# A halving moved from VectorE to ScalarE, and the later score units ordered by halves of the batch

## The chip, the cores and the metric

The kernel runs on one core of a Trainium2 chip. The metric is the device time of one execution in microseconds (us). Before the change three executions took 118.46 us in the median (117.84 to 118.76). The core has five engines that run programs of their own and meet only at semaphores: PE (TensorE, matrix products into PSUM), DVE (VectorE), ACT (ScalarE), POOL (GpSimd) and SP (SyncE, which here only issues DMAs).

## The reference

A batch of 4 sequences of 256 tokens with 256 features is normalised (no learned scale). The normalised activations go two ways. One is attention with 16 heads of 16 features, softmax over the whole sequence, and an output projection with a bias. The other is a feed-forward layer with 1024 hidden units, exact gelu, a second bias `proj2_bias`, and silu on its result. The output is the input plus the product of the two.

```python
xn  = _layernorm(x, axis=-1)
s   = attention(xn, Wqkv) @ Wproj.T + bproj        # 16 heads, softmax over 256 keys
h   = jax.nn.gelu(xn @ proj1.T + proj1_bias, approximate=False)
g   = _silu(h @ proj2.T + proj2_bias)
out = x + s * g
```

## The kernel before

Every product of full precision is split: an operand is a high part and a low part (names in `h` and `l`), and three products are summed (the low by low one is left out). So each operand is rounded to its high part on ACT, and the low part is the difference, taken on DVE or POOL.

The silu is computed through tanh: with y half of the layer's result, silu is y * (1 + tanh(y)). For that the second bias `b2s` is needed halved. It is loaded at the start and halved in place once. POOL is the first to use it (`early_sum`, L479), DVE the next (L810); both wait for the semaphore `b2_half`.

Scores are made twice. The first time (`S` units, PE L992) they only give row maxima. There are 32 such units: unit S(2n) and S(2n+1) are the two head pairs of `PAIRS[n]` = (j, b), where b is the sequence of the batch (0 to 3) and j a group of four heads (0 to 3). A unit is four matmuls into two banks of PSUM, and one DVE reduction over 1024 columns takes the maxima (L755). Units alternate between two pairs of banks, so S(n) waits on PE until the reduction of S(n-2) is done. When all four sequences of a group j have been reduced, DVE transposes the maxima (`MT`, L761), POOL splits them (L493, L495), and eight small DMAs write them as extra rows of q. The second scores (`ST` units, L1006) come with the maxima subtracted, ACT takes their exp (L640), and `PV` units (L1039) multiply by the values.

For both kinds of scores q and k must lie stacked in `qs` and `ks`. SP does this with 48 DMAs (L422) out of `stage`, in four packs of twelve, in this order: heads j = 0, 1 of sequences 0, 1; then of sequences 2, 3; then heads j = 2, 3 of sequences 0, 1; then of sequences 2, 3. Each pack has a semaphore `stacked[half of the batch][half of the heads]`. The first `S` unit that needs a pack waits for it on PE:

```python
if s[1] % 2 == 0 and (j, b) in ((0, 0), (0, 2), (2, 0), (2, 2)):
    pe.wait_ge(stacked[b // 2][j // 2], 192)
```

What PE does, unit by unit, is a list written by `build_order`: `PLAN` names the groups of first-layer (`F1`, named R1 in pieces), second-layer (`F2`, R2) and value units (`V`, RV), and behind which pieces of a group an `S` unit is put. The `S` units are dealt out by number, so `PAIRS` alone says which heads and sequence a number stands for. All engines walk the same list and pick their own steps from it. ACT's steps in the middle are the gelu of a first-layer unit (L623), its high part (`H`, L629), the values (L601), second-layer results (L664), and from ST0 on the exps. POOL makes the low parts `hTl` (L514). The step `("F1", 4)` stands behind S5 in the list; there DVE halves `b2s` (L751).

Of the kernel before, what the change touches and what calls it, by code (L numbers as in the profile page):

```python
# [5 lines left out]
B, SQ, E = 4, 256, 256  # L6
# [7 lines left out]
FC = F // P  # L14
# [34 lines left out]
LAST = GROUPS - B  # L49
CHUNKS = (0, 2, 1, 3)  # L50
PAIRS = ([(0, 0), (0, 1), (1, 0), (0, 2), (0, 3), (1, 1), (1, 2), (1, 3)]
         + [(j, b) for j in range(2, 4) for b in range(B)])


def members(kind, p, *part):
# [88 lines left out]
def layer_kernel(nc, x, wqkv, w1, b1, w2, b2, wp, bp, out):  # L144
    f32, f32r = mybir.dt.float32, mybir.dt.float32r
    ALU, ACT, AX = mybir.AluOpType, mybir.ActivationFunctionType, mybir.AxisListType
# [6 lines left out]
    with ctx:  # L153
        def sem(name):
            return ctx.enter_context(nc.semaphore(name))
# [7 lines left out]
        def at(name, shape, dtype, where=None):  # L163
            size = 4
            for n in shape[1:]:
                size *= n
            if where is None:
                where = used[0]
                used[0] += (size + 31) // 32 * 32
                assert used[0] <= slab * 4, (name, used[0])  # L170
            return nc.alloc_sbuf_tensor_at(name, shape, dtype, offset=base + where)
# [53 lines left out]
        b2s = at("b2s", [P, E], f32)  # L225
# [17 lines left out]
        w1_in, w2_in, wp_in, bias_in = (sem(n) for n in ("w1_in", "w2_in", "wp_in", "bias_in"))  # L243
# [20 lines left out]
        f2_made, f2_out, b2_half, yh_side, yh_done, yh_part, yh_pool, th_done, gate_done, gate_part, gate_pool, bg_done, xb_done = (  # L264
            sem(n) for n in ("f2_made", "f2_out", "b2_half", "yh_side", "yh_done", "yh_part", "yh_pool", "th_done",
                              "gate_done", "gate_part",
                              "gate_pool", "bg_done", "xb_done"))
# [295 lines left out]
        @block.scalar  # L563
        def _(act):
            act.wait_ge(warm_set, 1)
            nc.scalar.activation(rc[0:1, 0, 0:1], warm[0:1, 0:1], ACT.Gelu)

            def high_wqk(c):
                act.wait_ge(wqkv_in[c], 16)
                for q in range(2):  # L570
                    nc.scalar.activation(quarter(wqh, c, q), as_loaded(c, q), ACT.Copy).then_inc(wqk_hi, 1)

            high_wqk(0)
            n_qk = n_v = n_f1 = 0
            for s in order:
                if s[0] == "XT":
                    b = s[1]
                    act.wait_ge(xt_made, b + 1)
                    for kc in range(KC):
                        nc.scalar.activation(xTh[:, kc, b * SQ:(b + 1) * SQ], bank[:, home[("XT", b)][kc], 0:SQ],  # L580
                                             ACT.Copy).then_inc(xt_hi, 1)
                    if b == 0:
                        high_wqk(1)
                        act.wait_ge(wqkv_in[2], 16)
                        nc.scalar.activation(wqh[:, 2], wqkv_raw[:, 2], ACT.Copy).then_inc(wv_hi, 1)
                elif s[0] == "QK":
                    h, i = s[1:]
                    act.wait_ge(qk_made, n_qk + 1)
                    nc.scalar.activation(stage[:, h, i, 0, :], bank_of(*s), ACT.Copy,  # L589
                                         scale=SCALE if i < 2 else 1.0).then_inc(qk_hi, 1)  # L590
                    n_qk += 1
                    if n_qk in (2, 4):
                        act.wait_ge(w1_in, 16)
                        kc = n_qk // 2 - 1
                        nc.scalar.activation(w1h[:, kc, :], w1_raw[:, kc, :], ACT.Copy).then_inc(w1_hi, 1)  # L595
                elif s[0] == "V":
                    h, p = s[1:]

                    act.wait_ge(v_made, n_v + 1 if h == 0 else 4)
                    tt = 4 * h + 2 * p  # L600
                    nc.scalar.activation(VA[:, tt:tt + 2, :, 0:HN],  # L601
                                         bank_of(*s).rearrange("p (t n d) -> p t n d", t=2, d=HN),
                                         ACT.Copy).then_inc(v_out, 1)
                    n_v += 1
                elif s[0] == "F1":
                    f = s[1] % FC
                    if n_f1 == 0:
                        act.wait_ge(w2_in, 16)
                        for fs in (slice(0, 4), slice(4, 8)):
                            nc.scalar.activation(w2s[:, fs, 0, :], w2_in_place[:, fs, 1, :], ACT.Copy).then_inc(w2_hi, 1)  # L610
                        act.wait_ge(bias_in, 48)
                        act.wait_ge(xt_made, B)
                    if n_f1 == FC:
                        act.wait_ge(f2_made, TT // 2)
                        act.wait_ge(wp_in, 128)
                        act.wait_ge(stacked[1][0], 192)
                        act.wait_ge(stacked[1][1], 192)
                        nc.scalar.activation(wph[:], wps[:], ACT.Copy).then_inc(wp_hi, 1)

                        nc.scalar.activation(rc[0:1, 0, 0:1], b1s[0:1, 0:1], ACT.Gelu)  # L620

                    act.wait_ge(f1_made, 2 * (n_f1 // 2) + 2)
                    nc.scalar.activation(hG[:, f, :], bank_of(*s), ACT.Gelu,  # L623
                                         bias=b1s[:, f:f + 1]).then_inc(gelu_done, 1)
                    n_f1 += 1
                elif s[0] == "H":
                    f = s[1] % FC
                    act.wait_ge(gelu_done, s[1] + 1)
                    nc.scalar.activation(hTh[:, f, :], hG[:, f, :], ACT.Copy).then_inc(h_hi, 1)  # L629
                elif s[0] == "ST":  # L630
                    w = s[1]
                    act.wait_ge(st_made, w + 1)
                    if w < 4:
                        act.wait_ge(stacked[0][0], 192)
                        act.wait_ge(stacked[0][1], 192)
                    if 4 <= w < 8:
                        act.wait_ge(f1_made, 2 * FC)
                    if w >= 8:
                        act.wait_ge(pv_made, (w - 8) // 2 + 1)
                    nc.scalar.activation(exp_of(w), scores_of(*s), ACT.Exp).then_inc(exp_done, 1)  # L640
                elif s[0] == "MROWS":
                    maxima_rows(act, act, 0)
                elif s[0] == "TANH" and s[1] < EARLY:
                    u = s[1]
                    act.wait_ge(yh_pool, u + 1)
                    if u >= 2:
                        act.wait_ge(gate_part, u - 1)
                    nc.scalar.activation(th[:, u % 2, :], sums_of(u)[:, 0], ACT.Tanh).then_inc(th_done, 1)
                elif s[0] == "TANH":
                    u = s[1]  # L650
                    act.wait_ge(yh_done, u - EARLY + 1)
                    if u >= EARLY + 2:
                        act.wait_ge(gate_done, u - EARLY - 1)
                    else:
                        act.wait_ge(gate_pool, u - 1)
                    nc.scalar.activation(th[:, u % 2, :], yh[:, u % 2, :], ACT.Tanh).then_inc(th_done, 1)
                elif s[0] == "F2" and s[1] < EARLY:
                    u = s[1]
                    if u == 0:
                        act.wait_ge(v_made, 4)  # L660
                    act.wait_ge(f2_made, 2 * (u // 2) + 2)
                    if u >= 2:
                        act.wait_ge(gate_pool, u - 1)
                    nc.scalar.activation(sums_of(u).rearrange("p a e -> p (a e)"), bank_of("F2", u, 0), ACT.Copy,  # L664
                                         scale=0.5).then_inc(f2_out, 1)
            for u in BY_ACT:
                store(act, act, u)
# [3 lines left out]
        def _(dve):  # L671
# [52 lines left out]
            for s in order:  # L724
                if s[0] == "XT":
                    b = s[1]
# [13 lines left out]
                elif s[0] == "QK":  # L740
                    h, i = s[1:]
# [4 lines left out]
                    n_qk += 1  # L746
                    if n_qk == 1:
                        norm_apply(3)
                elif s == ("F1", 4):
                    dve.wait_ge(bias_in, 48)  # L750
                    nc.vector.tensor_scalar(b2s[:], b2s[:], 0.5, None, ALU.mult).then_inc(b2_half, 1)  # L751
                elif s[0] == "S":
                    j, b = PAIRS[s[1] // 2]
                    dve.wait_ge(s_made, s[1] + 1)
# [2 lines left out]
                elif s[0] == "MT":  # L757
                    j = s[1]
# [16 lines left out]
                elif s[0] == "PV" and s[1] in (t[-1] for t in TOGETHER):  # L775
# [15 lines left out]
                    for n, g in enumerate(groups):  # L791
                        j, b = divmod(g, B)
# [24 lines left out]
                elif s[0] == "TURN":  # L817
                    kc, j = s[1:]
# [278 lines left out]
```

## Time and profile before

| | |
|---|---|
| median of 3 executions | 118.46 us (117.84 to 118.76) |
| profiled execution, its own time | 117.66 us |
| its span | 115.9 us |
| PE busy | 110.4 us (95%) |
| DVE busy | 87.0 us (75%), 37.8 of them the 32 reductions of L755 |
| ACT busy | 75.8 us (65%) |
| POOL busy | 71.5 us (62%) |
| PE clock granted | full in every slice |

The span is the time from the first to the last instruction of the profiled execution; its own time has 1.8 us more around it, and lies 0.80 us under the median of the unprofiled ones. Times below are from the span's start. A row of the timeline gives the start, how long the merged piece lasted, the engine, line and tile, how often (x), and in brackets how long the engine sat idle before it and what ended that. PE is the product, PEld the load of its weights, and SPq the issuing of DMAs on SP.

### The profile page before, as it was taken

The numbers are of one execution on the slowest core, as the hardware profiler recorded it, in microseconds if no ns is written. First come the engines' busy times: TensorE is split into PE (matmuls) and PEld (weight loads), VectorE is DVE, ScalarE is ACT, GpSimd is POOL, SyncE is SP. The second block draws the span as 40 slices with busy tenths as digits, with TensorE's granted clock in tenths as the row PEclk, the third lists the DMA queues.
The fourth block names the chain that finished last, engine by engine and source line by source line (L and its number), as shares of the span: only waits on it lengthen the run. The fifth ranks groups of instructions, "written<-read, shape, count | busy, mean of one in ns | idle before, by whom it ended". The sixth has DMA issues, their size and how long they took to land.

```text
span 115.9 us, 2969 instructions
## 1 busy us (share of the span) xinstructions
PE 110.4 (95%) x1114; PEld 89.2 (77%) x1114; DVE 87.0 (75%) x158; ACT 75.8 (65%) x112; POOL 71.5 (62%) x92
## 2 busy tenths in 40 slices
PE   5889999999999999999999999999999999999990
PEld 4588998779986998898788888785866867566660
DVE  0799994537889988987598899043986868999862
ACT  5074795481986630397867887979968798799100
POOL 4227679039799930099748766999691581457480
PEclk9999999999999999999999999999999999999999
DMA  3999955465613564564000001700000000020214
GB/s 96 315 358 378 344 173 194 154 209 199 206 39 100 179 198 139 193 197 132 3 7 1 6 0 69 296 0 8 7 8 10 0 0 6 0 91 6 91 47 137
DMA packets 9634, 13.30 MB, mean 115 GB/s; under 512 B 2452, under 2 KB 4884, under 8 KB 9492
## 3 DMA queue, kind: packets, MB, share of 16 engines
q1 hardware_dynamic: 9060, 12.82, 33.6%
q10 hardware_dynamic: 560, 0.30, 0.9%
q8 instruction: 9, 0.15, 0.5%
q14 instruction: 5, 0.04, 0.1%
HBM read 5.51 MB, written 1.05 MB: 57 GB/s over the span
## 4 chain that ended last, share of the span: by engine, by line
PE 55%; SPq 30%; DMA 5%; issue 3%; DVE 2%; ACT 2%; POOL 1%; POOLq 0%
SPq L422 29%; PE bank L1039 13%; PE bank L979 10%; PE bank L864 9%; PE bank L1006 8%; PE bank L1022 7%; PE bank L1019 3%; PE bank L992 3%; DMA ks<-stage 2%; DMA xs<-x 2%; PE bank L1050 2%; SPq L411 1%; PE bank L898 1%; ACT stage L589 1%; ACT w1h L595 1%
## 5 line engine op out<-in xcount | busy, mean ns | idle before, releaser
L755 DVE TENSOR_REDUCE negm<-bank 128x4 f32<-128x1024 f32 x32 | 37.8, 1218 | 7.5 <-PE bank L992 7.4
L514 POOL TENSOR_TENSOR hTl<-hG,hTh 128x512 fp32r<-128x512 f32 x16 | 20.4, 1297 | 5.6 <-ACT hTh L629 5.6
L640 ACT ACTIVATE PT<-bank 128x1024 f32<-128x1024 f32 x16 | 15.6, 1026 | 2.8 <-PE bank L1006 2.7
L623 ACT ACTIVATE hG<-bank,b1s 128x512 f32<-128x512 f32 x16 | 10.7, 681 | 7.0 <-PE bank L979 7.0
L992 PEld LDWEIGHTS bank<-ks,qs 48*128 48x128 f32 x128 | 11.8, 186 | 2.7 <-DVE negm L755 0.7
L992 PE MATMUL bank<-ks,qs 48*128 48x256 f32 x128 | 13.3, 282 | 0.3 <-DVE negm L755 0.2
L1022 PE MATMUL bank<-w2s,hTh 128*128 128x512 f32 x32 | 11.9, 410 | 0.0
L979 PE MATMUL bank<-w2s,hTh 64*128 64x512 f32 x64 | 11.9, 398 | 0.0
L979 PE MATMUL bank<-xTh,w1l 64*128 64x512 f32 x64 | 11.2, 391 | 0.0
L1006 PEld LDWEIGHTS bank<-qs,ks 50*128 50x128 f32 x128 | 8.5, 185 | 3.4 <-issue 1.2
L1006 PE MATMUL bank<-qs,ks 50*128 50x256 f32 x128 | 11.0, 297 | 0.0
L979 PE MATMUL bank<-xTh,w1h 64*128 64x512 f32 x64 | 11.0, 416 | 0.0
L629 ACT ACTIVATE hTh<-hG 128x512 fp32r<-128x512 f32 x16 | 9.9, 634 | 0.4
L979 PE MATMUL bank<-xTl,w1h 64*128 64x512 f32 x64 | 10.1, 389 | 0.0
L640 ACT ACTIVATE PT_more<-bank 128x1024 f32<-128x1024 f32 x8 | 7.9, 1025 | 1.5 <-PE bank L1006 1.5
L640 ACT ACTIVATE PT_last<-bank 128x1024 f32<-128x1024 f32 x8 | 7.9, 1025 | 1.3 <-PE bank L1006 1.3
L979 PE MATMUL bank<-w2s,hTl 64*128 64x256 f32 x64 | 8.3, 278 | 0.0
L1019 PE MATMUL bank<-w2s,hTl 128*128 128x256 f32 x32 | 8.3, 280 | 0.0
L743 DVE SCALAR_TENSOR_TENSOR stage<-bank,stage 128x512 fp32r<-128x512 f32 x8 | 5.3, 685 | 3.7 <-ACT stage L589 3.7
L533 POOL TENSOR_TENSOR bg<-gate,bps 128x256 f32<-128x256 f32 x8 | 6.4, 805 | 2.5 <-DVE gate L710 2.5
L479 POOL TENSOR_TENSOR gate<-gate,b2s 128x256 f32<-128x256 f32 x4 | 3.0, 740 | 8.0 <-ACT gate L664 8.0
L786 DVE STREAM_TRANSPOSE cd<-bank 128x256 f32<-128x256 f32 x12 | 4.9, 434 | 4.0 <-PE bank L1039 3.9
(108 smaller groups left out, 256.2 us busy)
## 6 DMA issues: line engine op xcount, KB each, us to landing
qs<-stage SPq DMA_DIRECT2D x24, 128.0 KB, 2.9
ks<-stage SPq DMA_DIRECT2D x24, 128.0 KB, 2.9
xs<-x SPq DMA_DIRECT2D x4, 256.0 KB, 3.7
w_raw<-w SPq DMA_DIRECT2D x1, 1024.0 KB, 7.4
w_in_place<-w SPq DMA_DIRECT2D x1, 1024.0 KB, 10.0
xb<-x SPq DMA_DIRECT2D x1, 1024.0 KB, 5.0
wqkv_raw<-wqkv SPq DMA_DIRECT2D x3, 256.0 KB, 4.3
out<-fin SPq DMA_DIRECT2D x6, 128.0 KB, 1.8
```

The costliest lines, as they stand in the source:

```text
L422: sp.dma_start(stack[row:row + STK:3, 4 * q:4 * q + 4, cols].bitcast(f32), stage[64 * par:64 * par + 64, h, i, part, :].bitcast(f32)).then ...
L514: nc.gpsimd.tensor_tensor(hTl[:, n % FC, :], hG[:, n % FC, :], hTh[:, n % FC, :].bitcast(f32), ALU.subtract).then_inc(h_lo, 1)
L623: nc.scalar.activation(hG[:, f, :], bank_of(*s), ACT.Gelu, bias=b1s[:, f:f + 1]).then_inc(gelu_done, 1)
L640: nc.scalar.activation(exp_of(w), scores_of(*s), ACT.Exp).then_inc(exp_done, 1)
L755: nc.vector.tensor_reduce(negm[:, j, :, s[1] % 2, b, :], scores_of(*s), axis=AX.X, op=ALU.max, negate=True).then_inc(max_done, 1)
L864: m = nc.tensor.matmul(dst, lhs(kc, a), rhs(kc, b), start=first and n == 0, stop=last and n == len(todo) - 1)
L979: m = nc.tensor.matmul(dst, lhs, rhs, start=first and n == 0, stop=done and not begins)
L992: last = nc.tensor.matmul(scores_of(*s)[:, par, qt, :], qs[rows, hp, c:c + P], ks[rows, hp, b * SQ:(b + 1) * SQ], start=True, stop=True)
L1006: last = nc.tensor.matmul(scores_of(*s)[:, par, kt, :], ks[rows, hp, c:c + P], qs[rows, hp, b * SQ:(b + 1) * SQ], start=True, stop=True)
L1019: m = nc.tensor.matmul(bank_of("F2", u, 0)[:, 0:E], hTl[:, fc, c:c + P], w2s[:, fc, 0, :], start=False, stop=False)
L1022: m = nc.tensor.matmul(bank_of("F2", u, 0), hTh[:, fc, c:c + P], w2s[:, fc].rearrange("p a e -> p (a e)"), start=fc == 0, stop=fc == FC - 1)
L1039: last = nc.tensor.matmul(spot("PV", g)[32 * m:32 * m + VW, :], VA[:, 2 * b + kt, 4 * j + m, :], exp_of(w)[:, m % 2, kt, :], start=(kt == ...
```

## The change

Two edits. The halving of `b2s` is no longer a DVE instruction behind S5 but an ACT instruction (a copy with scale 0.5, in place) behind the high part of hidden unit 7. And `PAIRS` lists the last sixteen `S` units as heads j = 2, 3 of sequences 0, 1 and then j = 2, 3 of sequences 2, 3, where it had all of j = 2 and then all of j = 3.

```diff
 PAIRS = ([(0, 0), (0, 1), (1, 0), (0, 2), (0, 3), (1, 1), (1, 2), (1, 3)]
-         + [(j, b) for j in range(2, 4) for b in range(B)])
+         + [(j, b) for h in range(2) for j in range(2, 4) for b in (2 * h, 2 * h + 1)])
@@ ACT
                     nc.scalar.activation(hTh[:, f, :], hG[:, f, :], ACT.Copy).then_inc(h_hi, 1)
+                    if s[1] == FC - 1:
+                        nc.scalar.activation(b2s[:], b2s[:], ACT.Copy, scale=0.5).then_inc(b2_half, 1)
@@ DVE
-                elif s == ("F1", 4):
-                    dve.wait_ge(bias_in, 48)
-                    nc.vector.tensor_scalar(b2s[:], b2s[:], 0.5, None, ALU.mult).then_inc(b2_half, 1)
```

On DVE, from the first reduction (S0) to the last transpose of maxima, before:

```order
L755 TENSOR_REDUCE negm<-bank 128x2x2 [waits s_made] x6
L751 TENSOR_SCALAR b2s<-b2s 128x256 [waits bias_in]
L755 TENSOR_REDUCE negm<-bank 128x2x2 [waits s_made] x4
L761 STREAM_TRANSPOSE mt<-negm 128x32 [waits max_done]
L755 TENSOR_REDUCE negm<-bank 128x2x2 [waits s_made] x6
L761 STREAM_TRANSPOSE mt<-negm 128x32 [waits max_done]
L755 TENSOR_REDUCE negm<-bank 128x2x2 [waits s_made] x8
L761 STREAM_TRANSPOSE mt<-negm 128x32 [waits max_done]
L755 TENSOR_REDUCE negm<-bank 128x2x2 [waits s_made] x8
L761 STREAM_TRANSPOSE mt<-negm 128x32 [waits max_done]
```

and now:

```order
L754 TENSOR_REDUCE negm<-bank 128x2x2 [waits s_made] x10
L760 STREAM_TRANSPOSE mt<-negm 128x32 [waits max_done]
L754 TENSOR_REDUCE negm<-bank 128x2x2 [waits s_made] x6
L760 STREAM_TRANSPOSE mt<-negm 128x32 [waits max_done]
L754 TENSOR_REDUCE negm<-bank 128x2x2 [waits s_made] x12
L760 STREAM_TRANSPOSE mt<-negm 128x32 [waits max_done]
L754 TENSOR_REDUCE negm<-bank 128x2x2 [waits s_made] x4
L760 STREAM_TRANSPOSE mt<-negm 128x32 [waits max_done]
```

The halving between S5's and S6's reduction is gone, and the transpose of the maxima of j = 2 stands behind S27's reduction, no longer behind S23's.

On PE, the score units S20 to S24 in the middle of the program (each is one row with its wait and one row x3; the rows between are first-layer products), before:

```order
L992 MATMUL bank<-ks,qs 128x256 [waits max_done,stacked11]
L992 MATMUL bank<-ks,qs 128x256 x3
...
L992 MATMUL bank<-ks,qs 128x256 [waits max_done]
L992 MATMUL bank<-ks,qs 128x256 x3
L979 MATMUL bank<-xTh,w1h 128x512 [waits w1_lo,w1_hi,turn_made]
```

where the first two rows are S20 and the last three S24, and now, S20 and S24 again:

```order
L991 MATMUL bank<-ks,qs 128x256 [waits max_done]
L991 MATMUL bank<-ks,qs 128x256 x3
...
L991 MATMUL bank<-ks,qs 128x256 [waits max_done,stacked11]
L991 MATMUL bank<-ks,qs 128x256 x3
L978 MATMUL bank<-xTh,w1h 128x512 [waits w1_lo,w1_hi,turn_made]
```

The wait for the last pack of stacked q and k has moved from S20 to S24; nothing else of PE's program is in another place. On ACT the new instruction stands alone between two neighbours of before:

```order
L623 ACTIVATE hG<-bank,b1s 128x512 [waits f1_made]
L629 ACTIVATE hTh<-hG 128x512 [waits gelu_done]
L631 ACTIVATE b2s<-b2s 128x256
L601 ACTIVATE VA<-bank 128x32x16 [waits v_made] x2
L378 DMA qs<-mm 2x16x32 [waits m_lo,m_hi]
```

It waits for nothing of its own, and no load of an activation table has come in with it.

## Rows read from the trace of the kernel before

**Rows 1.** The page, the chain of work that ended last, by engine
```profile
PE 55%; SPq 30%; DMA 5%; issue 3%; DVE 2%; ACT 2%; POOL 1%; POOLq 0%
```

**Rows 2.** The same chain in order of time, 44 to 58 us: start, us, what
```profile
52.78 2.85 DMA ks<-stage
...
56.18 1.38 PE bank L979 x12
```

**Rows 3.** Waits of PE's weight loads, 20 to 75 us: total, times, longest
```profile
PEld bank L992 <- DVE negm L755: 0.7, 1, 0.7
PEld bank L992 <- DMA ks<-stage: 0.4, 1, 0.4
```

**Rows 4.** Timeline of PE; the L992 rows are S6, S8, S16, S19, S20, S31
```profile
34.82 0.41 PE L992 MATMUL bank<-ks,qs 48*128 48x256 f32 x4
...
36.36 0.63 PE L979 MATMUL bank<-xTl,w1h 64*128 64x512 f32 x4
37.24 0.50 PE L992 MATMUL bank<-ks,qs 48*128 48x256 f32 x4 [0.25 <-DVE negm L755]
37.58 0.41 PE L979 MATMUL bank<-wqh,xTh 64*128 64x256 f32 x4
...
48.73 0.40 PE L992 MATMUL bank<-ks,qs 48*128 48x256 f32 x4
...
49.93 0.41 PE L1006 MATMUL bank<-qs,ks 50*128 50x256 f32 x4
...
51.35 0.40 PE L979 MATMUL bank<-w2s,hTh 64*128 64x512 f32 x2
51.59 0.40 PE L992 MATMUL bank<-ks,qs 48*128 48x256 f32 x4
...
55.20 0.39 PE L979 MATMUL bank<-w2s,hTh 64*128 64x512 f32 x2
55.68 0.50 PE L992 MATMUL bank<-ks,qs 48*128 48x256 f32 x4
56.02 0.63 PE L979 MATMUL bank<-xTh,w1h 64*128 64x512 f32 x4
...
70.00 0.40 PE L992 MATMUL bank<-ks,qs 48*128 48x256 f32 x4
```

**Rows 5.** Timeline of DVE, 33 to 72 us, around the halving and the transposes
```profile
33.65 1.22 DVE L755 TENSOR_REDUCE negm<-bank 128x4 f32<-128x1024 f32 x1 [0.50 <-PE bank L992]
34.79 1.26 DVE L751 TENSOR_SCALAR b2s<-b2s 128x256 f32<-128x256 f32 x1
35.97 4.71 DVE L755 TENSOR_REDUCE negm<-bank 128x4 f32<-128x1024 f32 x4
...
61.35 0.21 DVE L761 STREAM_TRANSPOSE mt<-negm 128x32 f32<-128x32 f32 x1
61.49 1.19 DVE L755 TENSOR_REDUCE negm<-bank 128x4 f32<-128x1024 f32 x1
...
64.82 7.11 DVE L755 TENSOR_REDUCE negm<-bank 128x4 f32<-128x1024 f32 x6 [0.40 <-PE bank L992]
```

**Rows 6.** Timeline of ACT, 39 to 52 us
```profile
39.02 0.63 ACT L629 ACTIVATE hTh<-hG 128x512 fp32r<-128x512 f32 x1
41.04 1.09 ACT L601 ACTIVATE VA<-bank 128x512 f32<-128x512 f32 x2 [1.38 <-PE bank L979]
...
51.64 0.41 ACT L648 ACTIVATE th<-gate 128x256 f32<-128x256 f32 x1
```

**Rows 7.** Timeline of POOL, the low parts of the first eight hidden units
```profile
32.10 8.95 POOL L514 TENSOR_TENSOR hTl<-hG,hTh 128x512 fp32r<-128x512 f32 x7 [0.37 <-ACT hTh L629]
```

**Rows 8.** Timeline of SP, the last six DMAs of the third pack
```profile
39.62 4.84 SPq L422 DMA_DIRECT2D ks<-stage  x6
```

**Rows 9.** Issue to landing of the DMAs into ks
```profile
DMA to landing us min/median/max: 2.7/2.9/3.8
```

**Rows 10.** Packets of ACT's DMA queue (the eight of L378), 48.5 to 49 us
```profile
q10 hardware_dynamic: 22, 0.00, 3.4%
```

## The prediction, made before the changed kernel was run

> **What bounds the kernel now.** I read the chain of waits first, by engine and then in order of time. By engine it gives PE 55% and SP's queue 30% [rows 1]. That 30% is easily misread. The chain is followed backwards from the end; it goes along PE down to 55.68 us, jumps there to the landing of the last stacking DMA (52.78 + 2.85 = 55.63), and follows SP's queue from there on [rows 2, 4]. So the queue is not what PE waited for all that time; it says that for some 35 us (30% of 115.9) SP issued one DMA after the other, and that PE had to stop for the last of them at one point. How long it stopped is in the waits of PE's weight loads: between 20 and 75 us there are two stops worth naming, 0.7 us for a DVE reduction and 0.4 us for that DMA [rows 3]. Otherwise PE has its next instruction ready throughout this stretch. The time is PE's own work plus its stops, and the change can only touch the stops.
>
> The timeline of PE puts the first stop at S8 (37.24) and the second at S20 (55.68) [rows 4]. S8 needs the banks that the reduction of S6 frees. The DVE timeline shows why that one was late: S5's reduction ends at 34.87, then the halving of `b2s` takes DVE until 36.05, although S6's product was there at 34.82 + 0.41 = 35.23 [rows 4, 5].
>
> **Part 1, the halving leaves DVE.** S6's reduction can start at about 35.25 where it started at 35.97. Four reductions in a row took 4.71 us, 1.18 each [rows 5], so it ends at 36.43 and not at 37.15. What PE gets of that: the piece before S8 starts at 36.36 and has four matmuls, which take a third of the 1.38 us of twelve, 0.46 [rows 2, 4]. S8 would start at 36.82. A score unit of four matmuls with 256 columns goes through in the time of two with 512, which is 0.24 (51.35 to 51.59) [rows 4]. The work behind S8 would start at 37.06; it started at 37.58. That is **0.52 us**. Bounds: 0.25, the idle time that the product row itself shows, and 0.7, that of the weight loads [rows 3, 4]. I take the spacing of the starts, since it holds what PE in fact issued later. The loads had been released at the end of the reduction, 37.15, after 0.7 us of idling [rows 3], so PE wanted S8's banks at about 36.5, 0.3 before the product. At 36.43 they are free by then, and I leave no rest of the wait.
>
> Why did 256 columns take 1.26 us on DVE, longer than a reduction over 1024? POOL had seven equal operations without a gap from 32.10 on, 8.95 / 7 = 1.28 each [rows 7]; one of them ran from 34.66 to 35.94, and the halving came free just then. The Trainium skill (SBUF — State Buffer, section SBUF: two separate sides) says that DVE in a mode that uses both ports and GpSimd take a shared pair of ports exclusively, for a whole instruction, the other blocking. By that rule the trace agrees, and the length depends on where in a POOL operation the halving falls. From the skill's table of cycles (VectorE: DVE Perf Modes, section on the TRN2 errata) I work out an estimate of 0.2 us for it undisturbed; at that length it would never have delayed S6, and the sum would lose the 0.52. The row says 1.26, and the row decides.
>
> **Part 2, S20 no longer needs the last pack.** In the new list S20 to S23 are heads j = 3 of sequences 0 and 1, which are in the third pack, the one that S16 has already waited for. S20 would have started at 55.20 + 0.24 = 55.44, and the work behind it at 55.68; it started at 56.02 [rows 4]. That is **0.34 us**; bounds 0.24 (the shift of S20's own start) and 0.4 [rows 3]. The last pack's landing is set by SP alone, so it stays at 55.63. The wait is now at S24, whose reduction started at 61.49 [rows 5], so some 5 us after the landing; it costs nothing even 0.9 us earlier.
>
> The two parts depend on each other. With part 1 alone PE would be at S20 0.52 us sooner and would wait that much longer for the same landing. Only with both does the sum 0.86 reach the end.
>
> **Part 3, the halving on ACT.** It follows the last high part, which ends at 39.65, ahead of the values, for which ACT sat idle 1.38 us until 41.04 [rows 6]. PE is 0.52 earlier now, so 0.87 us of cover is left. The price: a 256-column ACT operation took 0.41 [rows 6]; the dearest bound is the 1.26 that DVE needed [rows 5]. At 0.41 it is hidden; at 1.26 the values come 0.4 late. Queued behind them on ACT are the eight DMAs of L378, but these wait for POOL, whose row of low parts ends at 41.05 as before [rows 7]. I cost it at nothing at either end. Its users, POOL's first sum and DVE's much later one, come after second-layer work that PE finishes only about S16, 48 us [rows 4].
>
> **Part 4, the transpose of the j = 2 maxima moves behind S27.** It takes between 0.14 (start to next start) and 0.21 us [rows 5]. Where it stood, DVE was not urgent. Where it goes, six reductions run back to back from 64.82, 1.18 each [rows 5]; S29's ended at 69.56, and S31, which needs its banks, started its product at 70.00 [rows 4] and so wanted them at 69.7. The margin is 0.14 and the transpose takes 0.14 to 0.21. I take **0.02 us** lost, with 0 and 0.07 as ends. What hangs on the maxima of j = 2 (POOL's split, SP's rows) comes after POOL's second row of low parts, and ST16, the user, is late in the program.
>
> **What PE meets on its way, being earlier.** At S16 the third pack: its last six issues end at 39.62 + 4.84 = 44.46 [rows 8]. The last began about 0.8 earlier, and a landing takes 2.9 (at most 3.8) [rows 9], so it lands at 46.6, at the latest, counted from the end of the issue, 48.3. S16's product moves from 48.73 to 48.21 [rows 4]. At ST0 the eight rows of j = 0: ACT's queue still had packets after 48.5, none after 49 [rows 10]; ST0 moves from 49.93 to 49.41, its wait to 49.1. Both hold, the second by 0.1 us or a bit more. After S31 no DMA that runs by itself stands in the way: the exps, the sums and the reload of x all start from PE's products, so I let the gain pass to the end.
>
> **Sum.** -0.52 - 0.34 + 0.02 = **-0.84 us**. The profiled execution took 117.66; it becomes 116.82. The median of the runs is 0.80 above the profiled one, so I forecast 118.46 - 0.84 = **117.6 us**.
>
> **Rivals.**
>
> *Given back at a DMA.* PE's 0.52 from part 1 is lost at S16 or ST0, because the pack or the rows land later than my middle value; or S6's reduction doesn't come that much sooner. For it: the margin of 0.1 at ST0, and the upper bound of 48.3 at S16. Against: the median landing leaves 1.4 us at S16. Part 2 stays: -0.34, 118.1 us. Chance 0.20.
>
> *The stop at S20 is longer in most executions than in the profiled one.* That execution is 0.80 us under the median and under the lowest of the three. If those 0.80 lie in SP's chain of issues, the usual stop at S20 is 0.34 + 0.80 = 1.14, and the change removes it all: -0.52 - 1.14 + 0.02 = -1.64, 116.8 us. For it: the chain hung on SP for a third of the time, and its issues have no slack between them. Against: nothing shows where the scatter is; and a third pack that is over 1.4 us late would stop PE at S16. Chance 0.28.
>
> *Slower: DVE becomes the bound in S26 to S31.* Place: the six reductions, now with the transpose among them. It decides from 0.14 us of DVE lateness on, past which each tenth is lost by PE. The price, if the slip is as large as one reduction: 1.18 + 0.21 - 0.14 = 1.25 lost against 0.86 won, +0.39, 118.85 us; two reductions of slip would make it more than 1%. For it: that stretch has no idle DVE time at all. Against: DVE starts it after an idle 0.40 of its own, waiting for PE [rows 5], and PE's own order there is unchanged. Chance 0.06.
>
> *No effect at all,* since the halving's place or the wait's were not the real cause: both rows name their releaser directly, and the new order has the wait at S24; 0.04 for this and what I don't see. My forecast itself gets 0.42.
>
> **Range and chances.** The forecast's own range is 117.2 to 118.0. Reaching to the rival given back (118.1) and to the larger gain (116.8), with a few tenths for the median of few runs: 116.6 to 118.4. A difference of less than 1%, 1.18 us, can't be told from none here. Faster by more than that: nearly all of the larger gain and a tail of the forecast, 0.34. Slower by more: 0.05, from the larger slip of DVE and from what I don't see. Within: 0.61.
>
> **What would show it.** On DVE: reductions of S0 to S9 with nothing between, S6's starting within 0.1 us of its product's end. On PE: no idle before S8, none before S20, the fourth pack's wait unseen at S24. S31's product 0.8 to 0.9 us earlier than 70.00, and the end by the same amount. A new stop at S16 or ST0 would show the first rival, an idle PE before S28 to S31 with DVE as releaser the third. It is wrong in its main line if PE is earlier at S31 by what I say and not at the end: then something behind 70 us that I let follow PE has a clock of its own.

## The result

The changed kernel takes 117.1 us in the median (22 runs, 116.76 to 117.94), the kernel before in the same sessions 118.09 us (22 runs, 117.23 to 119.26). The ratio is 0.9938, 95% interval 0.9918 to 0.9958: 0.73 us faster (0.50 to 0.97). The ratio leaves out as slow the runs that are more than 1.5% above the fastest of their kernel, four of before's 22 (119.06 to 119.26), and so it gives 0.73 us where the medians of all runs differ by 0.99. Forecast were -0.84 us and 117.6 us, with a range of 116.6 to 118.4, and a change of less than 1% as the likeliest outcome. Size, sign and this range held; the narrower range that the forecast called its own, 117.2 to 118.0, missed 117.1 by 0.1, where the kernel before itself came out 0.37 under the 118.46 that the forecast started from. The way there failed in one place: a stop of PE that the prediction had at nothing. The number came out right all the same; what made up for the stop is not fully shown.

The profiled execution of the changed kernel took 117.61 us, its span was 115.8 us, so it is hardly shorter than the profiled one of before (117.66, 115.9). The two are not alike as samples: this one lies 0.51 us above the median of its 22 runs, that of before 0.43 below its own. The chain of waits, by engine:

```profile
PE 84%; DMA 5%; ACTq 4%; DVE 2%; ACT 1%; issue 1%; POOL 1%; POOLq 0%
```

SP's queue, 30% in [rows 1], is gone from it, and 4% of ACT's queue is new. The waits of PE's weight loads, 20 to 75 us, tell what happened (total, times, longest):

```profile
PEld bank L1005 <- DMA qs<-mm: 0.6, 1, 0.6
PEld bank L978 <- issue: 0.4, 1, 0.4
```

Both stops of [rows 3] are gone. There is a new one of 0.6 us, for the rows of maxima at ST0 (the 0.4 us of "issue" stands in the trace of before too). PE's timeline; the rows of L991 are S6, S8, S17, S20, S24, S30 and S31, that of L1005 is ST0:

```profile
35.03 0.40 PE L991 MATMUL bank<-ks,qs 48*128 48x256 f32 x4
...
37.02 0.40 PE L991 MATMUL bank<-ks,qs 48*128 48x256 f32 x4
37.26 0.40 PE L978 MATMUL bank<-wqh,xTh 64*128 64x256 f32 x4
...
49.37 0.40 PE L991 MATMUL bank<-ks,qs 48*128 48x256 f32 x4
50.21 0.50 PE L1005 MATMUL bank<-qs,ks 50*128 50x256 f32 x4 [0.44 <-DMA qs<-mm]
50.55 0.39 PE L978 MATMUL bank<-w2s,hTh 64*128 64x512 f32 x2
...
55.48 0.40 PE L978 MATMUL bank<-w2s,hTh 64*128 64x512 f32 x2
55.71 0.41 PE L991 MATMUL bank<-ks,qs 48*128 48x256 f32 x4
55.96 0.63 PE L978 MATMUL bank<-xTh,w1h 64*128 64x512 f32 x4
...
60.96 0.40 PE L991 MATMUL bank<-ks,qs 48*128 48x256 f32 x4
...
69.00 0.41 PE L991 MATMUL bank<-ks,qs 48*128 48x256 f32 x4
...
69.94 0.40 PE L991 MATMUL bank<-ks,qs 48*128 48x256 f32 x4
```

Against [rows 4]: this execution was 0.21 late already at S6, where nothing has changed (in the four profiled executions of before S6 starts between 34.82 and 35.16). The work behind S8 is 0.32 early, so 0.53 was won there. The work behind ST0 is late again: it would have started 0.24 + 0.24 after S17, at 49.85, and started at 50.55, 0.70 later. Behind S20 it stands at 55.96 against 56.02. The DMA that held ST0, in the chain in order of time, and the packets of its queue from 48.5 to 49 us (there are none from 49 to 49.5):

```profile
46.94 3.23 DMA qs<-mm
...
50.21 0.50 PE bank L1005 x4
```

```profile
q10 hardware_dynamic: 34, 0.00, 7.2%
```

On DVE the halving is gone and S6's reduction follows its product; the transpose of j = 2 stands in the row of reductions:

```profile
33.84 1.23 DVE L754 TENSOR_REDUCE negm<-bank 128x4 f32<-128x1024 f32 x1 [0.52 <-PE bank L991]
35.47 3.49 DVE L754 TENSOR_REDUCE negm<-bank 128x4 f32<-128x1024 f32 x3 [0.40 <-PE bank L991]
...
64.77 2.36 DVE L754 TENSOR_REDUCE negm<-bank 128x4 f32<-128x1024 f32 x2 [0.40 <-PE bank L991]
67.16 0.21 DVE L760 STREAM_TRANSPOSE mt<-negm 128x32 f32<-128x32 f32 x1
67.30 4.58 DVE L754 TENSOR_REDUCE negm<-bank 128x4 f32<-128x1024 f32 x4
```

and on ACT it takes 0.40 us, with idle time behind it:

```profile
39.76 0.40 ACT L631 ACTIVATE b2s<-b2s 128x256 f32<-128x256 f32 x1
40.72 1.09 ACT L601 ACTIVATE VA<-bank 128x512 f32<-128x512 f32 x2 [0.56 <-PE bank L978]
```

### The profile page after: what moved, and what is told of

Same layout as the page of the kernel before. It is cut to its first block, busy times and chain, and to the rows that moved or that the text cites. A ratio compares the mean times of both kernels' runs of the same rounds, so it can differ in the third digit from the quotient of the medians.

```text
span 115.8 us, 2969 instructions
## 1 busy us (share of the span) xinstructions
PE 110.5 (95%) x1114; PEld 88.9 (77%) x1114; DVE 86.0 (74%) x157; ACT 76.1 (66%) x113; POOL 71.3 (62%) x92
## 4 chain that ended last, share of the span: by engine, by line
PE 84%; DMA 5%; ACTq 4%; DVE 2%; ACT 1%; issue 1%; POOL 1%; POOLq 0%
PE bank L978 26%; PE bank L863 17%; PE bank L1038 13%; PE bank L1005 9%; PE bank L1021 7%; PE bank L991 5%; ACTq L378 4%; PE bank L1018 3%; DMA qs<-mm 3%; DMA xs<-x 2%; PE bank L897 2%; PE bank L1049 2%; ACT VA L601 1%; DVE stats L678 1%; POOL rstd L450 1%
## 5 line engine op out<-in xcount | busy, mean ns | idle before, releaser
L991 PEld LDWEIGHTS bank<-ks,qs 48*128 48x128 f32 x128 | 11.6, 186 | 2.1
L991 PE MATMUL bank<-ks,qs 48*128 48x256 f32 x128 | 12.9, 279 | 0.0
L1005 PEld LDWEIGHTS bank<-qs,ks 50*128 50x128 f32 x128 | 8.5, 185 | 4.1 <-issue 1.2
L1005 PE MATMUL bank<-qs,ks 50*128 50x256 f32 x128 | 11.1, 297 | 0.4 <-DMA qs<-mm 0.4
L500 POOL TENSOR_TENSOR w2s<-w_in_place,w2s 128x1024 fp32r<-128x1024 f32 x2 | 4.8, 2396 | 5.0 <-ACT w2s L610 5.0
```

The source lines that it names most:

```text
L991: last = nc.tensor.matmul(scores_of(*s)[:, par, qt, :], qs[rows, hp, c:c + P], ks[rows, hp, b * SQ:(b + 1) * SQ], start=True, stop=True)
L1005: last = nc.tensor.matmul(scores_of(*s)[:, par, kt, :], ks[rows, hp, c:c + P], qs[rows, hp, b * SQ:(b + 1) * SQ], start=True, stop=True)
```

## The experiments

Ratios are to the kernel before on the same chip, with their 95% interval.

### Each part alone

`halving_only` is the changed kernel with the old list of score units:

```diff
-         + [(j, b) for h in range(2) for j in range(2, 4) for b in (2 * h, 2 * h + 1)])
+         + [(j, b) for j in range(2, 4) for b in range(B)])
```

> The halving of the second bias sits on ScalarE, the score units keep their order of before. My account: PE is 0.52 us earlier from S8 on, loses that again at ST0 (waits for the rows of maxima) or at S20 (waits for the last pack of stacked q and k, landing at about 55.6 us), so the time is that of before, ratio 0.998 to 1.002. The rival 'the halving alone makes the gain' wants a ratio near 0.994 and no stop at S20.

Measured: 117.62 us, ratio 0.9983 (0.9948 to 1.0019). No difference that can be told. Its PE waits:

```profile
PEld bank L991 <- DMA ks<-stage: 0.6, 1, 0.6
PEld bank L1005 <- DMA qs<-mm: 0.2, 1, 0.2
```

S8 has no stop, and what is won there goes to a small stop at ST0 and a longer one at S20, whose product starts at 55.68 as in [rows 4].

`pairs_only` is the kernel before with the new list alone.

> The score units go by halves of the batch, the halving stays on VectorE behind S5. By my sum of one profiled execution only 0.34 us is gained (ratio 0.997) and the 0.52 of S8 stays lost. The rival 'in most executions the stop at S20 is longer than in the profiled one' wants most of the gain of the whole change here, 0.6 to 1.0 us (0.992 to 0.995), and less scatter between runs than the kernel before has. ST0 should not be stopped, since PE is not early.

Measured: 117.42 us (117.0 to 117.78), ratio 0.9962 (0.9938 to 0.9985): 0.45 us. The stop at S8 is there, those at S20 and ST0 are not:

```profile
PEld bank L992 <- DVE negm L755: 0.7, 1, 0.7
```

Between the 0.34 of one profile and the 0.6 to 1.0 of the rival this does not decide: the interval (0.18 to 0.73) holds the first and the lower third of the second. On the scatter the rival was right. The runs lie in 0.78 us, those of before in the same session in 2.0 us (117.19 to 119.20, with two far longer ones apart), and those of `halving_only`, which keeps PE's wait at S20, in 1.87.

### What the halving costs on VectorE where GpSimd is idle

`halving_dve_quiet` is the changed kernel with the halving back on DVE, behind another reduction:

```diff
-                    if s[1] == FC - 1:
-                        nc.scalar.activation(b2s[:], b2s[:], ACT.Copy, scale=0.5).then_inc(b2_half, 1)
@@ behind the reduction
+                    if s[1] == 12:
+                        dve.wait_ge(bias_in, 48)
+                        nc.vector.tensor_scalar(b2s[:], b2s[:], 0.5, None, ALU.mult).then_inc(b2_half, 1)
```

> The new order of score units, and the halving on VectorE again, but behind S12, where GpSimd has nothing to do. If the 1.26 us of before were a wait for the ports that GpSimd held, it takes 0.2 to 0.35 us here; if it is the price of the operation on VectorE, 1.26 again. Time as the changed kernel in the first case (0.993 to 0.995); in the second up to 0.5 us more if PE runs into the reduction of S14.

Its DVE timeline:

```profile
44.47 0.28 DVE L756 TENSOR_SCALAR b2s<-b2s 128x256 f32<-128x256 f32 x1
```

The same instruction takes 0.28 us here and took 1.26 in [rows 5]. In all six traces that have it behind S5 it takes 1.23 to 1.26 us and ends some 0.1 us after the end of one of POOL's low parts (at 36.05 in [rows 5], where POOL's third operation of the row ends at 32.10 + 3 * 1.28 = 35.94). The time is 117.06 us, ratio 0.9929 (0.9902 to 0.9956), as the changed kernel, with a stop of 0.4 us at ST0 like it. So what counted was to take the halving from under POOL's low parts; ScalarE is one way to do it, another place on VectorE is as good.

### The rows of maxima at ST0

`rows_shared` is the changed kernel with two of the eight row DMAs of j = 0 issued by SP (m = 3), between its third and fourth pack, and six by ACT:

```diff
-        def maxima_rows(engine, queue, j):
+        def maxima_rows(engine, queue, j, ms=range(4)):
...
-            for m in range(4):
+            for m in ms:
...
                 for h in range(2):
+                    if (q, h) == (1, 1):
+                        maxima_rows(sp, sp, 0, (3,))
...
-                    maxima_rows(act, act, 0)
+                    maxima_rows(act, act, 0, range(3))
```

> The changed kernel, with two of the eight small DMAs that write the maxima of j = 0 issued by SP between the third and the fourth pack of stacking DMAs, six by ScalarE. My account of the changed kernel's trace: PE stops 0.6 us at ST0 for the last of these rows. ScalarE's last issue would start 1.3 us earlier, so the stop goes: 0.5 to 0.6 us less than the changed kernel, ratio to before 0.989. SP's fourth pack comes 1.2 us later, landing at about 56, which S24 at 60 does not feel. If something else behind ST0 sets the end, the ratio stays at 0.994.

Measured: 116.88 us (116.67 to 117.14), ratio 0.9916 (0.9886 to 0.9946), seven runs; the profile has no stop at ST0. The expected 0.989 lies at the interval's lower end. A second measurement has the changed kernel beside it:

> The changed kernel again, beside the next one: ratio to before 0.991 to 0.996, a stop of 0.3 to 0.7 us at ST0 for the rows of maxima, none at S8 and S20.

> Two of the eight rows of maxima issued by SP, again, beside the changed kernel: 0.2 to 0.6 us less than it, the spread of its runs no wider than 0.6 us, no stop at ST0. The rival, that the difference of the first time was one between executions, wants the medians within 0.1 us of each other.

| | median us | range of 12 runs | ratio (95%) | stop at ST0 in the profile |
|---|---|---|---|---|
| `after_again` | 117.33 | 116.73 to 117.88 | 0.9954 (0.9922 to 0.9987) | 0.4 us |
| `rows_shared_again` | 116.79 | 116.69 to 117.53 | 0.9927 (0.9897 to 0.9958) | none |

PE's timeline of `rows_shared_again`; ST0, and the work behind S20 and S31 as in [rows 4]:

```profile
35.01 0.40 PE L993 MATMUL bank<-ks,qs 48*128 48x256 f32 x4
...
49.53 0.40 PE L1007 MATMUL bank<-qs,ks 50*128 50x256 f32 x4
...
55.29 0.63 PE L980 MATMUL bank<-xTh,w1h 64*128 64x512 f32 x4
...
69.27 0.40 PE L993 MATMUL bank<-ks,qs 48*128 48x256 f32 x4
```

Here the forecast's sum can be read without the new stop. S6 is 0.19 late against before and the work behind S20 0.73 early: 0.92 won, where 0.86 was forecast for the two stops. S31 is 0.73 early, and the profiled execution (116.85 us) 0.81 shorter than before's 117.66. What PE wins before 70 us does reach the end. This version is the fastest measured: medians of 116.88 and 116.79. Against the changed kernel of the same session its median is 0.54 us lower; the two ratios differ by less (0.3%) and their intervals overlap. Eleven of its twelve runs are at 117.10 us or less, and only two of the changed kernel's twelve. So that it is faster is fairly clear; the size of the step stays open, while its cause, the stop, is seen to go. One run of the twelve, 117.53, lies outside the 0.6 us that were expected for their spread.

### Delays of SP's chain, made on purpose

Two DMAs into a spare buffer, issued by SP ahead of the fourth pack, in the kernel before (`old_order_late_pack`) and in the changed one (`new_order_late_pack`):

```diff
                 for h in range(2):
+                    if (q, h) == (1, 1):
+                        for n in range(2):
+                            sp.dma_start(spare[:, n, :], bp[:, 0:16].to_broadcast([P, 16])).then_inc(spare_in, 16)
```

> The kernel before with two more small DMAs (into a spare buffer that nobody reads) that SP issues ahead of the fourth pack of stacking DMAs. If S20's wait passes every delay of SP's chain on to the end, the pack lands about 1.2 us later (two issues of 0.6) and the time grows by the same 1.2, ratio 1.010; the stop at S20 is then 1.5 us or so. If there is slack that the profile did not show, less.

> The changed kernel with the same two DMAs ahead of the fourth pack. S24 wants the pack at 60 us and gets it at 57: no stop, the time is that of the changed kernel, ratio to before 0.992 to 0.996. If the wait still binds at S24, or ScalarE's wait for the same pack (ahead of the high part of the projection's weights) delays the gelu, up to 0.5 us more.

Old order: 118.67 us, ratio 1.0074 (1.0031 to 1.0117), 0.87 us more; the 1.2 us expected lies inside the interval. Its profiled execution was the longest of its eleven runs, 121.41 us, with a stop of 2.6 us at S20, so the 1.5 expected there is not shown. It shows one thing more. PE sat idle 2.32 us until S20 at 58.02, and behind it the granted clock fell: 0.64 between 59 and 60 us, 0.50 (the lower level, 1.2 GHz) from 60 to 62, 0.66 to 63, and full again. From S20 to S24 it took 6.78 us, where [rows 4] and the start of S24 at 61.01 give 5.33. The row of S20 and the page's row of the clock:

```profile
58.02 0.51 PE L998 MATMUL bank<-ks,qs 48*128 48x256 f32 x4 [2.32 <-DMA ks<-stage]
```

```profile
PEclk9999999999999999999959999999999999999999
```

New order: 117.10 us (116.86 to 118.4), where the changed kernel of the same session had 117.33; the ratio to before is 0.9974 (0.9935 to 1.0012), not the 0.992 to 0.996 expected, though the interval holds that too. Eight of the ten runs are at 117.53 or below, within the range of the changed kernel, and two at 118.4. So the delay of the fourth pack costs nothing in most runs, and no wait for it shows at S24. The wait that the profile shows is again at ST0, in one of the two long executions (118.38 us):

```profile
PEld bank L1011 <- DMA qs<-mm: 1.4, 1, 1.4
```

Here the last row of maxima landed 4.50 us after its issue began, and the last packets of ACT's queue came at 49.9, not before 49.0:

```profile
46.36 4.50 DMA qs<-mm
```

Whether the two added DMAs delayed these packets, or they come late now and then in the changed kernel too, is not shown; in its own two profiled executions the stop at ST0 was 0.6 and 0.4 us.

### Where the scatter of the kernel before lies

Three more profiled executions of the kernel before:

> The kernel before, unchanged, profiled once more. If the scatter of its times comes from the stop at S20, that stop differs between looks by as much as the times do (0.4 us at 117.7 us, 1 us or more at 118.3 and above), while the stop at S8 stays at 0.7. If it comes from elsewhere, the stop at S20 stays at 0.3 to 0.5.

> The kernel before a second time, for the same two readings: the stop at S20 grows with the time of the execution, or it stays at 0.3 to 0.5 us whatever the time is.

> The kernel before a third time, for the same two readings: the stop at S20 grows with the time of the execution, or it stays at 0.3 to 0.5 us whatever the time is.

| | time us | stop at S8 | stop at S20 |
|---|---|---|---|
| `before_look_2` | 117.43 | 0.7 | 0.3 |
| the first one of before ([rows 3]) | 117.66 | 0.7 | 0.4 |
| `before_look_1` | 117.76 | 0.7 | 0.4 |
| `before_look_3` | 119.05 | 0.7 | 1.6 |

The waits and the chain of `before_look_3`:

```profile
PEld bank L992 <- DMA ks<-stage: 1.6, 1, 1.6
PEld bank L992 <- DVE negm L755: 0.7, 1, 0.7
```

```profile
54.35 2.76 DMA ks<-stage
...
57.15 0.51 PE bank L992 x4
```

The last pack landed at 57.11, not at 55.63, since its last issue started at 54.35 and not at 52.78; the time from issue to landing was as before. Against `before_look_2` that is 1.3 us more of stop and 1.62 us more of time; S6 was 0.27 later already, which is the rest, and S31 is 1.63 later. The granted clock stayed full behind this stop. This is a reading of one long execution out of four, not a distribution.

## Why the prediction was right, and where it was not

**Part 1, 0.52 us for the halving's leaving DVE: right in mechanism and size, at its place.** 0.53 at S8. The dependence on POOL, argued from the boundaries in [rows 7], is shown by `halving_dve_quiet`. The Trainium skill (SBUF — State Buffer, section SBUF: two separate sides) has the rule that a VectorE instruction in a two-port mode and a GpSimd one exclude each other for a whole instruction. By that rule, the trace agrees: 0.28 us alone, 1.26 under POOL.

**Part 2, 0.34 us for S20: right for the profiled execution; whether it is too small for the usual one stays open.** It was read from an execution that took 0.43 us less than the median of 22. In a long one the stop is 1.6 us, and none of the seven profiles with the new order has any wait for that pack. That is the mechanism of the rival "the stop at S20 is longer in most executions", whose price of -1.64 in all was too high; "most" was not shown (three of four profiled executions have 0.3 to 0.4), and `pairs_only` puts the effect at 0.45 us with an interval, 0.18 to 0.73, that holds 0.34.

**The two parts depend on each other: shown by the trace.** In `halving_only` PE is early behind S8 and starts S20 at 55.68, as before; its time gains nothing that can be measured (-0.61 to +0.22 us).

**The check of ST0 was the step that failed.** The prediction had the margin at "0.1 us or a bit more", reading the last packets of ACT's queue before 49.0 [rows 10] as the landing. The landing was later: in the changed kernel the last packets are before 49.0 too, and PE was released at 50.17, some 1.2 us after. The last of the eight issues starts at 46.94 and lands 3.23 us after. In `after_again`, `halving_dve_quiet` and `new_order_late_pack` the release comes 0.9 to 1.0 us after the last packets. With 0.9 to 1.2 us added, the last packets of before (48.7) mean a landing at 49.6 to 49.9, an estimate: ST0's wait at 49.1 had no margin but a stop of 0.5 us or more ahead of it, and the sum had this at nothing. The rows of SP's DMAs [rows 9] would have told it: at most 3.8 us from issue to landing. The Trainium skill (DMA: Bandwidth & Descriptors, section Anatomy of one DMA — SWDGE (gpsimd) path, so of DMAs that GpSimd issues) says that most of a DMA's fixed 2 us is the receipt of the write, after the bytes. This DMA is of ACT's path, but its 1.2 us between last packet and release point the same way. The rival "given back at a DMA" named the place and a price of up to 0.52; it had 0.20 and should have had more. In three profiled executions with the changed list, the halving on ACT and all eight rows there, the stop was 0.6, 0.4 and 1.4 us (the last with SP's two more DMAs).

**Part 3 and part 4: right.** ACT took 0.40 us under 0.96 us of cover (39.76 to 40.72). S30 to S31 is 0.94 us before and after, so the transpose among the reductions cost nothing, and the rival in which DVE becomes the bound is out.

**So the sum.** One term was missing: the stop at ST0, 0.4 to 0.6 us in the profiles. Put into the sum it gives -0.24 to -0.44, and -0.73 was measured, so something made up for it. Candidates are a stop at S20 that is longer than 0.34 in the usual execution of before, and a stop at ST0 that is shorter in most executions than in the profiled one, which lay 0.51 above its median. No run separates them. That the total came out near -0.84 is in part luck. Without the stop, in the `rows_shared` pair, the ratios stand for 0.99 and 0.86 us, close to the 0.84 forecast.

## What to carry to other kernels

A margin before a DMA's landing must be taken to its semaphore, from issue-to-landing times or from a wait, not to its last packet. A stop that one profile prices at 0.3 us can be the place where executions differ: look at the profiled time against the median, profile again, and prefer the order that takes the wait off a chain with no slack. When one engine gets earlier, list the external arrivals that it will now meet, and fix the next one in the same step, as the shared rows do here.

## What the runs showed of the hardware that was not expected

- A 128x256 float32 multiplication by a constant on VectorE, SBUF to SBUF, took 0.28 us with GpSimd idle and 1.23 to 1.26 in six traces while GpSimd ran elementwise operations of 1.28 us back to back, each time ending some 0.1 us after one of these.
- A small DMA of ACT's queue (4 KB) released its waiter 3.23 us after its issue began, 1.2 us after its queue's last packets; in three other traces it was 2.96, 3.00 and 4.50 us after the issue began and 0.9 to 1.0 us after the last packets.
- In `old_order_late_pack` PE was idle for 2.32 us until 58.02, the granted clock was 0.50 from 60 to 62 us and full again from 63; after the stop of 1.6 us in `before_look_3` it stayed at 1.00. One trace each.
- SP's issues, mostly 0.60 us each, stretch now and then. Where the chain lists them singly past 40 us (`before`, `before_look_1`, `before_look_3`, `halving_only`, `old_order_late_pack`), one of them takes 1.64 to 2.19 us and starts between 41.55 and 42.54, about when ACT begins to issue (41.63 to 41.92). Of the packs of six in the changed kernel the first row below overlaps the beginning of ACT's issues (41.80 on), the second most of the rest of them, the third none:

```profile
39.16 4.81 SPq L422 DMA_DIRECT2D ks<-stage  x6
44.07 4.05 SPq L422 DMA_DIRECT2D qs<-stage  x6
48.22 4.19 SPq L422 DMA_DIRECT2D ks<-stage  x6
```

A single issue took 1.37 us in `before_look_3` and 2.11 us in `old_order_late_pack` with ACT's queue silent, so ACT's issuing can't be the only cause. What stretches an issue was not tried and stays open.
